# A dense two-layer graph network on one core: the corner of the transposed adjacency kept on chip in the first aggregation, and shorter row loads for blocks 0 to 3

## What is computed

```python
def _L0_gnn_ref(x, adj, W1, b1, W2, b2):
    def _gcn_norm_dense(adj):
        n = adj.shape[0]
        A = adj + jnp.eye(n, dtype=adj.dtype)
        deg = A.sum(axis=1)
        d = jnp.where(deg > 0, jax.lax.rsqrt(deg), 0.0)
        return d[:, None] * A * d[None, :]
    An = _gcn_norm_dense(adj)
    h = jax.nn.relu(An @ (x @ W1) + b1)
    return An @ (h @ W2) + b2
...
x = _layernorm(x + _L0_gnn_ref(x, adj, W1, b1, W2, b2), axis=-1)
x = _layernorm(x + _L1_gnn_ref(x, adj, ff0_w, ff1_w, attn_w, g1, b1, g2, b2), axis=-1)
```

## Time and profile before

| | us |
|---|---|
| median of three runs | 1020.89 |
| the profiled execution, as timed | 1018.46 |
| its span in the profile | 1015.4 |
| first product of the first aggregation | 22.28 |
| hidden layer's first product (`times_w2`) | 265.65 |
| second aggregation begins | 278.20 |
| PE busy over the span | 964.3 |

### The profile page before, as it was taken

The page is one execution under the profiler, slowest core; times in us unless marked ns, Lnnn a source line. Parts: engine busy times, 40 slices in busy tenths (PEclk is TensorE's granted clock), DMA queues, the critical chain, the costliest instruction groups (busy, mean ns, idle before and its releaser), DMA issues. The chain is left out here.

```text
span 1015.4 us, 9241 instructions
## 1 busy us (share of the span) xinstructions
PE 964.3 (95%) x2492; PEld 453.9 (45%) x2492; DVE 725.1 (71%) x1313; ACT 492.1 (48%) x756; POOL 187.1 (18%) x193
## 2 busy tenths in 40 slices
PE   5988989999999999999999999999999999999993
PEld 4333334444644444444555454444444444444541
DVE  1777766766565443426888777888779999888977
ACT  5343333221200000000088768778676888978774
POOL 1212223233059000004710001000000001010013
PEclk8999999999999999999999999999999999999997
DMA  9999999999579999993232232223212233313311
GB/s 380 419 420 419 418 417 417 415 417 399 243 288 381 379 395 377 387 392 149 87 102 80 65 94 72 94 62 104 68 57 93 84 104 94 104 63 94 94 52 42
DMA packets 69297, 223.88 MB, mean 220 GB/s; under 512 B 5318, under 2 KB 44806, under 8 KB 56710
## 3 DMA queue, kind: packets, MB, share of 16 engines
q1 hardware_dynamic: 65280, 209.67, 54.7%
q10 hardware_dynamic: 3974, 13.73, 3.4%
HBM read 203.43 MB, written 19.96 MB: 220 GB/s over the span
## 5 line engine op out<-in xcount | busy, mean ns | idle before, releaser
L1460 PE MATMUL ps<-T,Yw 128*128 128x512 f32 x1024 | 444.6, 593 | 1.0 <-DVE T L1107 0.6
L1460 PE MATMUL ps<-colbuf,stat 128*128 128x512 f32 x832 | 367.9, 602 | 23.3 <-DVE stat L899 23.3
L1133 DVE SCALAR_TENSOR_TENSOR T<-T,mring 128x2048 f32<-128x2048 f32 x125 | 286.0, 2289 | 63.2 <-ACT T L663 62.6
L663 ACT ACTIVATE T<-Rrow,small,ratio 128x1024 f32<-128x1024 f32 x250 | 294.8, 1231 | 61.5 <-PE ps L1460 61.3
L1460 PEld LDWEIGHTS ps<-T,Yw 128*128 128x128 f32 x1024 | 193.8, 190 | 237.9 <-issue 229.6
L1460 PEld LDWEIGHTS ps<-colbuf,stat 128*128 128x128 f32 x832 | 158.3, 192 | 228.9 <-issue 205.4
L582 ACT ACTIVATE W<-W 128x896 f32<-128x896 f32 (+15 forms) x57 | 67.9, 1191 | 136.1 <-DMA W<-in_adj 135.7
L961 DVE TENSOR_SCALAR mtile<-colbuf 128x4096 uint8<-128x4096 f32 x28 | 65.9, 2355 | 36.9 <-DMA mask<-mtile 36.2
L600 ACT ACTIVATE stat<-xw_g 128x128 f32 x20 | 6.2, 309 | 158.8 <-PE ps L1460 145.8
L524 POOL TENSOR_SCALAR rs<-sumsq 128x4 f32<-128x4 f32 x14 | 15.1, 1078 | 322.6 <-ACT squares L710 322.6
L471 POOL PARTITION_ALL_REDUCE colrow<-W x31 | 33.3, 1075 | 184.8 <-DVE W L860 164.4
(11 more groups left out here) (198 smaller groups left out, 682.5 us busy)
## 6 DMA issues: line engine op xcount, KB each, us to landing
colbuf<-in_adjT SPq DMA_DIRECT2D x64, 1024.0 KB, 16.7
colbuf<-in_adjT SPq DMA_DIRECT2D x24, 2048.0 KB, 10.5
mring<-mask SPq DMA_DIRECT2D x128, 256.0 KB, 2.7
mask<-mtile ACTq DMA_DIRECT2D x26, 512.0 KB, 10.1
W<-in_adjT SPq DMA_DIRECT2D x4, 2048.0 KB, 11.0
Rrow<-s_src SPq DMA_DIRECT2D x9, 512.0 KB, 4.1
W<-in_adj SPq DMA_DIRECT2D x4, 960.0 KB, 15.4
W<-in_adj SPq DMA_DIRECT2D x4, 896.0 KB, 16.0
```

Source lines behind the costliest of these rows:

```text
L663: last = act.activation(T[:, c % TS, j, :], Rrow[:, g % 2, :], ACT.Relu, scale=ratio[:, c * JB + j:c * JB + j + 1], bias=small[:, 8:9])
L1133: v.scalar_tensor_tensor(out=tile, in0=tile, scalar=1.0, in1=mring[:, c % TS, :, :].rearrange("p b n -> p (b n)"), op0=ALU.add, op1=ALU.mu ...
L1460: return pe.matmul(*args, skip_group_check=True, **kw)
```

## The change

A new buffer `corner` holds the first 512 columns (4 blocks, `CB`) of the first 16 blocks (`CR`) of `adjT`: 4.19 MB. It is loaded in two halves of 8 blocks right behind `xT`, and stays until the first 16 blocks are aggregated. The loads of `colbuf` for blocks 0 to 15 leave these 512 columns out, and PE takes bank 0 of these blocks from `corner`. Since `corner` holds everything that rows 0 to 511 have in columns 0 to 2047, the row loads of blocks 0 to 3 start at column 2048, whatever b is. DVE sums the corner instead: once over the first 8 blocks for all 512 columns (a reduction over the block index, into `corner_part`), then for each of the four blocks over the last 8 blocks for its 128 columns, plus an addition. `add_rest` for the first blocks begins at column 512. The chain through POOL now also runs for block 0.

```diff
-        mtile = sb("mtile", [P, 2, N], U8, first)
...
+        corner_part = Rrow[:, 0, 0:CB * P]
+        colrow = Rrow[:, 1, 0:2 * P].rearrange("p (s c) -> p s c", s=2)
+        colown = Rrow[:, 1, 2 * P:3 * P]
...
+        held = ExitStack()
+        corner = sb("corner", [P, CR, CB * P], F32, held)
+        held.close()
+        mtile = sb("mtile", [P, 2, N], U8, first)
...
         def row_parts(b):
-            lo, mid = b * P, (b + (B - b) // 2) * P
+            from_block = CR if b < CB else b
+            lo, mid = from_block * P, (from_block + (B - from_block) // 2) * P
...
         def near(b):
+            if b < CR:
+                return slice(CB * P, N // 2), slice(N // 2, N)
...
+            for k in range(CP):
+                sp.dma_start(corner[:, cols(k, CR // CP), :], corner_cols[:, cols(k, CR // CP), 0:CB * P]).then_inc(corner_loaded[k], 16)
...
-            for b in range(1, B):
-                pool.wait_ge(colown_done, b)
+            for b in range(B):
+                pool.wait_ge(colown_done, b + 1)
...
-                before, rest = (b - 1) % RING, slice((b + 1) * P, N)
+                before, rest = (b - 1) % RING, slice(max(b + 1, CB) * P, N)
...
+            def over_corner(out, rows, columns, done):
+                v.tensor_reduce(out, corner[:, rows, columns].rearrange("p j n -> p n j"), AX_X, ALU.add).then_inc(done, 1)
+
+            def corner_sums(b):
+                own = cols(b)
+                over_corner(colacc[:, own], slice(CR // CP, CR), own, corner_summed)
+                v.wait_ge(corner_summed, b + 2)
+                v.tensor_tensor(colacc[:, own], colacc[:, own], corner_part[:, own], ALU.add).then_inc(colown_done, 1)
+
+            v.wait_ge(corner_loaded[0], 16)
+            over_corner(corner_part[:, :], slice(0, CR // CP), slice(0, CB * P), corner_summed)
+            v.wait_ge(xw_done, NG)
+            v.wait_ge(corner_loaded[1], 16)
+            corner_sums(0)
             for b in range(B):
...
+                if b >= CB:
...
+                elif b + 1 < CB:
+                    corner_sums(b + 1)
+                v.wait_ge(colrow_ready, b + 1)
...
             def aggregate_halves(u, turn, b):
+                if b < CR:
+                    multiply(ps[:, 0, :], stat[:, u, :], block_of(corner, turn * RING + u), start=False, stop=False)
```

More of the change, by code:

```diff
@@ L209, in build @@
             "first_loaded consts skip_loaded ident_ready zeros_ready skip_step skip_ready")
+        corner_loaded = [sem(f"corner_loaded{k}") for k in range(CP)]
+        corner_summed = sem("corner_summed")
         near_loaded = [sem(f"near_loaded{s}") for s in range(RING)]
@@ L847, in _ @@
+            v.wait_ge(corner_loaded[0], 16)
[3 more added lines that the diff above has]
+            corner_sums(0)
             for b in range(B):
                 u = b % RING
[L849 to L853, removed]
+                before, own = (b - 1) % RING, cols(b)
+                if b >= CB:
+                    if b == CB:
+                        v.wait_ge(near_loaded[before], 16 * ((b - 1) // RING + 1))
@@ L854, in _ @@
                     if b == HB2:
                         v.wait_ge(col_loaded[before], 16 * ((b - 1) // RING + 1))
-                    if b == 1:
-                        v.tensor_copy(colacc[:, own], colbuf[:, before, own]).then_inc(colown_done, 1)
-                    else:
-                        v.wait_ge(colacc_done, b - 1)
-                        v.tensor_tensor(colacc[:, own], colacc[:, own], colbuf[:, before, own], ALU.add).then_inc(colown_done, 1)
-                    v.wait_ge(colrow_ready, b)
@@ L869, in _ @@
-                v.wait_ge(colpart_step, 3 * b + 1)
+                    v.wait_ge(colacc_done, b - 1)
+                    v.tensor_tensor(colacc[:, own], colacc[:, own], colbuf[:, before, own], ALU.add).then_inc(colown_done, 1)
+                elif b + 1 < CB:
+                    corner_sums(b + 1)
+                v.wait_ge(colrow_ready, b + 1)
+                v.tensor_tensor(colown[:, :], colrow[:, b % 2, :], ident[:, :], ALU.mult).then_inc(colpart_step, 1)
+                v.wait_ge(colpart_step, 3 * b + 1)
@@ L895, in _ @@
                 v.wait_ge(xw_ready, b // RING + 1)
-                v.wait_ge(near_loaded[u], 16 * (b // RING + 1))
-                own = colbuf[:, u, cols(b)]
+                if b < CB:
+                    own = corner[:, b, cols(b)]
+                else:
+                    v.wait_ge(near_loaded[u], 16 * (b // RING + 1))
+                    own = colbuf[:, u, cols(b)]
                 v.tensor_tensor(own, own, ident[:, :], ALU.add)
@@ L1495, in aggregate_halves @@
                     for k in groups:
-                        last = multiply(ps[:, k, :], stat[:, u, :], colbuf[:, u, cols(k, GW)], start=False, stop=False)
+                        if k > 0 or b >= CR:
+                            last = multiply(ps[:, k, :], stat[:, u, :], colbuf[:, u, cols(k, GW)], start=False, stop=False)
                 last.then_inc(pe_block, 1)
```

31 lines of the change are left out of this document (17 added, 14 removed).

## The result

The changed kernel takes 1016.27 us (median of 19 runs, 1012.49 to 1018.72), the kernel before 1021.63 us in the same comparison (19 runs, 1017.76 to 1024.62). The ratio is 0.9947, 95% interval 0.9934 to 0.9959: some 5.4 us (0.5%) faster, 4.2 to 6.7 by the interval. The forecast was 1014.9 us. The profiled execution of after took 1012.49 us with a span of 1010.7, where the sum against the profiled execution had given 1012.5; that they agree to 0.01 us is luck, since 1012.49 is the lowest of the 19.

What follows compares the result with a forecast made beforehand. The prediction took DVE and the load queue, nearly level, to bound the kernel until block 16, then PE. The phase ends 6.0 us earlier: 1018.46 - 6.0 = 1012.5 profiled, 1014.9 on the median of 1020.89; range 1009.4 to 1022.0.

Steps and rivals of the forecast that it cites:

- What bounds the kernel, and where: First aggregation: queue and DVE nearly level until block 16, DVE with about 0.7 us of room per block; then PE.
- The queue's saving, 9.05 us: Row loads of blocks 0 to 3 lose 3.80 MB; at 0.42 MB per us, 9.05 us off everything from block 16.
- The corner's arrival, 13.6 and 18.6: At the start, the corner's two halves were to land at 13.6 and 18.6 us, row 0 at 21.2.
- Rival (b): The corner's load arrives slowly, at half the rate in runs of 2 KiB: 1023.2 us, chance 0.11.
- The reduction, 1.6 ns an element: DVE's strided corner reductions: 1.6 ns, middle of 1.04 and 2.2; 6.7 us the first, 1.8 the others.
- (a): The stride of DVE's corner reductions is free, 1.04 ns an element: gain 8.9 us, 1012.0 us, chance 0.27.
- (c): DVE's corner reduction costs more than the loads save: at 3.2 ns an element 1028.0 us, chance 0.08.
- The chain on DVE: DVE's degrees: first at 25.6 us, block 4's at 58.4 (start costs 3.5 us), block 16's at 151.7 instead of 156.91.
- the sum of 93.3: DVE, blocks 5 to 16: 12 x 4.89 us plus 34.6 for their `add_rest`, without waits, makes 93.3 us.
- The end of the phase, and after: First aggregation ends 6.0 us earlier, with PE the bound from block 16; all later work moves with PE's end.
- Nothing of the 6.0 us is taken back: After the first aggregation: PE runs the second without a gap, so the whole 6.0 us was to remain.
- Rival (d): PE already set the pace at blocks 5 to 16, so only the late start counts: 1022 us, chance 0.09.

Runs made afterwards that it cites:

- e4_slow_dve: The kernel before, with a memset of 1536 elements added on DVE behind `add_rest` of blocks 5 to 16; 1027.31 us, ratio 1.0072.
- e3_fullrows: The changed kernel, with the dropped columns of row blocks 0 to 3 (3.80 MB) still loaded but not read; 1022.30 us, ratio to before 1.0015.
- e1_contig: The changed kernel, with every reduction over the corner reading as many elements from adjacent addresses; 1012.82 us, ratio to before 0.9913.
- e7_longruns: The changed kernel, with the corner's two transfers of the same size read in 16 KB runs, not 2 KB pieces; 1014.79 us.
- e6_steps: The changed kernel, with six extra DVE reductions of 512 elements at steps of 4 bytes to 2 KiB before the hidden layer; 1016.43 us, one run.
- e2_twice: The changed kernel, with the first reduction over the corner done twice in a row; 1022.20 us, ratio to before 1.001.

## Why the prediction was right, point by point

**What bounds the kernel, and where.** Right. DVE and the queue were nearly level before (8.9 us of room between the degrees of blocks 4 and 16, by e4_slow_dve), DVE was last after, and PE took over late. The forecast had PE bound from block 16; it was block 15, because the gap ahead of each block shrinks as `add_rest` gets shorter. That is worth nothing visible: 259.58 against 259.7.

**The queue's saving, 9.05 us.** The bytes are worth that (9.07 us between e3_fullrows and the changed kernel), but the sum put the cost of holding the corner at nothing, and it is 1.29 us. So the queue came 7.78 us earlier at row block 16, 147.05 where the forecast had 145.8. In the changed kernel this could not be seen in the time, since DVE was last; in e1_contig, where the queue is last again, the hidden layer came 7.7 us earlier than before. About 1 us of the 1.29 is what the corner lost on arrival. e3_fullrows shows that these bytes are the whole gain.

**The corner's arrival, 13.6 and 18.6.** Mis-sized: 14.2 and 19.7. The second half is read from e1_contig, where DVE waits for it (14.19 and 19.60; in the changed kernel the first reduction hides it), and that is 2.10 MB in 5.4 us or 0.388 MB per us, where the prediction had used 0.42 for all of the queue., which spoke against a slow corner, are of a stretch in which runs of many sizes are mixed; e7_longruns puts a third to a half of the loss on the runs of 2 KiB. Rival (b), half the rate, is ruled out.

**The reduction, 1.6 ns an element.** Slightly mis-sized: 1.71, well inside the bounds of 1.04 and 2.2. The Trainium skill's 1.73 ns for a source that hops 4 KiB at each element, in "Vector Engine (DVE) Microarchitecture Reference", section "Measured stream behaviour on trn2", was closer than the middle of the two bounds. It is given for another instruction; the runs here show 1.71 for this one, at 2 KiB. The row that had spoken for a free stride, L1166 with 8 elements, was no evidence: at 0.7 ns more for an element, 8 of them add 6 ns, and the row itself spreads from 156 to 165 ns. Rivals (a) and (c) fall with the 1.71.

**The chain on DVE.** The first degree came 0.9 us later than forecast (0.7 from the corner, 0.5 from the first reduction, less a little), block 4's only 0.15 later. The steps from block 0 to block 3 were 0.2 to 0.3 us shorter each than the sum had them; the parts were taken from a round with a wait for POOL in it, and POOL's wait is absent in these blocks (28 waits for 32 blocks). L892 takes 0.28 us there and 0.62 where it has waited, in block 4. From block 4 to 16 the sum of 93.3 stands against 93.1. Two errors of opposite sign, 0.9 and 0.75, thus made the match at block 16 better than its parts were.

**The end of the phase, and after.** 6.0 us forecast, 6.07 measured, and 6.13 at the first product of `T` (518.60 to 512.47). "Nothing of the 6.0 us is taken back" holds for the change, but as a claim on a single execution it is too strong: between 440 and 520 us an execution can lose up to 5 us to late loads and the clock, whatever came before. In the pair of profiles another 1.4 us went further on, 4.7 of 6.1 being left at the end, and the traces show where. The lead is still 6.13 us at a product near 780 us, ahead of which PE is idle alike in both. PE before and after, and the stage table of after:

```profile
785.20 2.00 PE L1460 MATMUL ps<-mixed,numS 128*128 x8 [2.37 <-DVE A L1196]
```

```profile
779.07 3.67 PE L1493 MATMUL ps<-mixed,numS 128*128 x8 [2.36 <-DVE A L1229]
```

```profile
780.00:785.00 5.00, 5.00 (x13) 3.15 (x12) 4.73 (x10) 2.89 (x6) 0.00 (x0) 0.75 0.20 56
```

The same eight products took 2.00 us in before, at a granted clock of 1.00, and 3.67 in after, where the clock was 0.91 in 775 to 780 and 0.75 in 780 to 785. Behind it the lead is 4.46 us (787.03 to 782.57); part of that is made up, and at PE's last product it is 5.41 (997.20 to 991.79). At the products `numS` from 592 us on, before this one, the lead is 6.11 or 6.12 us each time, at those behind it 5.32 to 5.42. So 0.7 us of the 1.4 is lost in this one place. The other 0.7 us goes behind PE's last product; why, no run shows.

**The forecast's number.** 1014.9 against 1016.27. Of the 1.4 us, 0.7 is that three runs of before gave a median of 1020.89 and 19 gave 1021.63; the rest is 5.4 for 6.0, inside the interval of the comparison. Rival (d), that the saving doesn't reach the end, is ruled out by e3_fullrows. The range, 1009.4 to 1022.0, holds the time of no change as well, so that the median lies in it says little; the marks along the trace, and the four runs that moved them, say more.

## What to carry to other kernels

When two chains are nearly level, size the one that is not being relieved: here it took 3 of the 9 us that the bytes were worth, and its late start went through undiminished. A reduction over the outer index of a block should not be read with a step of 16 bytes or more from element to element; halving additions over adjacent elements did the same sum in 60% of the time. And a row with few elements is no evidence for a price per element: multiply the suspected price by the elements first, and see whether the result stands out of the row's own spread.

## What the runs showed of the hardware

- A DVE reduction of float32 costs 1.04 ns an element with adjacent elements and 1.71 with a step of 2 KiB. In probes of 512 elements it took 0.68 us at steps of 4 and 8 bytes and 1.01 to 1.08 us at 16, 32 and 64 bytes and 2 KiB. So a step of two elements is free and one of four is not.
- The same 2.10 MB landed 0.4 us sooner in runs of 16 KiB than in runs of 2 KiB (13.72 against 14.08 us on the same chip, one profile each).
- A DVE memset of 1536 float32 took 1.34 us and had 0.27 us of issue time ahead of it.
- The granted clock fell to 0.50 for five us near 505 us in one execution and stayed at 1.00 in another over the same work, at a cost of up to 3.4 us (e6_steps, e2_twice).
- Behind 2.36 us without work the same eight products of PE took 3.67 us in one execution and 2.00 in another; the granted clock around them was 0.91 and 0.75 in the one, 1.00 in the other.
